# MLP matmuls in array tiles, and the ELU on two PSUM banks at once

## What is computed

```python
x = x + _L0_conv_ref(_gn(x), ...)   # 3x3 convolution, kernel mixed per sample from 3 experts
x = x + _L1_conv_ref(_gn(x), ...)   # abs, then a depthwise 3x3 convolution
x = x + _L2_conv_ref(_gn(x), 8)     # 17x17 box mean
x = x + _L3_conv_ref(_gn(x), ...)   # sum of 8 neighbours, then an MLP for each pixel
```

```python
nbr = _neighbor_sum(x_cat)
xn = jnp.repeat(nbr, 8, axis=1)
h = elu(w1 @ xn); h = elu(w2 @ h); h = elu(w3 @ h); h = elu(w4 @ h)
F_int = w5 @ h                      # then means over groups of 4, times 0.1
```

## Time and profile before

| | |
|---|---|
| median of three executions | 961.74 us |
| span of the profiled execution | 960.3 us |
| the profiled execution's own time | not listed apart from its span |
| PE busy | 827.8 us, 86% |
| DVE busy | 760.5 us, 79% |
| ACT busy | 628.2 us, 65% |
| POOL busy | 227.6 us, 24% |

### The profile page before, as it was taken

How to read it: one execution, slowest core, us unless ns; L and a number is a source line. 1 busy time by engine, 2 the same in 40 slices (tenths; PEclk the granted TensorE clock), 3 DMA queues, 4 the chain that set the end, 5 groups by cost and what they waited for, 6 DMA issues and landing times.

```text
span 960.3 us, 9306 instructions
## 1 busy us (share of the span) xinstructions
PE 827.8 (86%) x2391; PEld 397.9 (41%) x2391; DVE 760.5 (79%) x1267; ACT 628.2 (65%) x1105; POOL 227.6 (24%) x296
## 2 busy tenths in 40 slices
PE   2759786688999899998999899989998998979993
PEld 1423443353444345443445344444444452424330
DVE  2645674767989888988888898989897689878994
ACT  1020213476877768696878787787878687978883
POOL 2030143111512115122412151213312122221000
PEclk9979887988999999999999999999999899999997
DMA  5425423414020320214020402032112002001201
GB/s 97 77 43 93 86 37 71 88 23 74 8 61 16 59 38 17 60 24 72 16 60 16 67 13 62 15 58 38 34 44 47 17 17 61 16 16 41 54 16 44
DMA packets 68751, 43.18 MB, mean 45 GB/s; under 512 B 5602, under 2 KB 62306, under 8 KB 68722
## 3 DMA queue, kind: packets, MB, share of 16 engines
q1 hardware_dynamic: 66976, 42.57, 23.0%
q10 hardware_dynamic: 1746, 0.27, 0.2%
HBM read 9.67 MB, written 8.39 MB: 19 GB/s over the span
## 4 chain that ended last, share of the span: by engine, by line
PE 34%; DVE 28%; ACT 13%; DMA 10%; issue 6%; SPq 5%; POOL 2%; DVEq 0%; ACTq 0%; POOLq 0%
PE pz L700 17%; DVE g L908 8%; PE pc L644 6%; DMA xs<-in_x_dram 5%; ACT u L577 5%; ACT u L586 5%; DMA halo<-y 4%; DVE bn L828 4%; SPq L395 3%; DVE box_sum L961 3%; DVE u L903 3%; PE pc L659 3%; DVE box_sum L946 2%; ACT u L583 2%; PE pc L672 2%
## 5 line engine op out<-in xcount | busy, mean ns | idle before, releaser
L700 PE MATMUL pz<-g,wT 128*128 128x512 f32 x768 | 362.6, 611 | 11.7 <-DVE g L908 9.6
L577 ACT ACTIVATE u<-pz,s_row 128x512 f32<-128x512 f32 x354 | 241.6, 686 | 123.2 <-PE pz L700 121.9
L908 DVE SCALAR_TENSOR_TENSOR g<-pz,k_row,u 128x512 f32<-128x512 f32 x348 | 247.4, 744 | 57.2 <-ACT u L586 55.7
L586 ACT ACTIVATE u<-u 128x512 f32<-128x512 f32 x472 | 286.5, 635 | 1.3
L700 PEld LDWEIGHTS pz<-g,wT 128*128 128x128 f32 x768 | 144.9, 194 | 203.2 <-issue 113.2
L828 DVE BATCH_NORM_STATS2 bn<-xs 128x6 f32 (+1 forms) x128 | 87.1, 688 | 29.7 <-DMA xs<-in_x_dram 19.8
L696 PE MATMUL pz<-stack,w1T 128*128 128x512 f32 x256 | 83.8, 448 | 20.2 <-DMA stack<-near_rest 12.8
L659 PE MATMUL pc<-y,t 128*128 128x512 f32 x192 | 93.5, 625 | 5.2 <-DVE t L365 5.2
L669 PE MATMUL pc<-y,t 128*128 128x512 f32 x192 | 92.7, 620 | 2.4 <-ACT y L551 2.4
L577 ACT ACTIVATE u<-pz 128x512 f32<-128x512 f32 x118 | 68.2, 602 | 39.8 <-PE pz L696 39.8
L908 DVE SCALAR_TENSOR_TENSOR g<-pz,u 128x512 f32<-128x512 f32 x128 | 81.9, 683 | 11.3 <-ACT u L586 10.3
(11 more groups left out here) (118 smaller groups left out, 785.2 us busy)
## 6 DMA issues: line engine op xcount, KB each, us to landing
halo<-y SPq DMA_DIRECT2D x96, 120.0 KB, 3.3
xs<-in_x_dram SPq DMA_DIRECT2D x8, 1024.0 KB
stack<-near_rest SPq DMA_DIRECT2D x64, 128.0 KB, 2.3
out_dram<-xs SPq DMA_DIRECT2D x8, 1024.0 KB
stack<-stack SPq DMA_DIRECT2D x32, 128.0 KB, 2.2
halo<-y SPq DMA_DIRECT2D x48, 8.0 KB, 2.6
g<-in_con_late_dram SPq DMA_DIRECT2D x1, 712.5 KB, 9.6
con<-in_con_early_dram SPq DMA_DIRECT2D x1, 272.5 KB, 14.7
```

Source lines behind the costliest of these rows:

```text
L577: act.activation(u[:, m, :], pz[:, m, :], ACT.Relu, scale=-1.0, bias=s_row[:, l - 1:l] if l else 0.0).then_inc(relu_done, 1)
L586: act.activation(u[:, m, :], u[:, m, :], ACT.Exp, scale=-1.0).then_inc(exp_done, 1)
L700: pe.matmul(pz[:, m, :], wT[:, l - 1, :], g[:, m, :], start=True, stop=True).then_inc(z_mm, 1)
L908: dve.scalar_tensor_tensor(out=elus(j, q, l)[:, m, :], in0=pz[:, m, :], scalar=k_row[:, l - 1:l] if l else 1.0, in1=u[:, m, :], op0=ALU.ad ...
```

## The change

Layer 1 reads `near` itself: four float32 matmuls whose weights and data lie on 32 partitions each, one for each bank. The split on POOL, the three DMAs for each chunk, and the tiles `stack` and `near_rest` are gone. Layers 2 to 4 use the 64 by 64 weights without the zero blocks: for each pair of banks four matmuls, one in each quadrant of the array. Hidden vectors therefore change places between two banks in each layer. The output layer is four matmuls of 64 columns in two column groups, two of them adding to the other two.

The ELU works on a pair of banks (128 by 1024): relu, exp, relu, exp on ACT and two joins on DVE for each layer, with one semaphore step for each pair. `clips`, and the carrying of a join into the next chunk that went with it, are gone. The last layer's joins always write a tile of their own, `g_last`. The box and the neighbour sums share one pair of `band_part` tiles. DVE's `output` stands behind the joins of the next chunk's first layer everywhere.

```diff
-            def layer(j, q, l):
-                for m in range(M):
-                    if l == 0:
...
-                        if m == 0:
-                            pe.wait_ge(stack_in, STACK * (Q * j + q + 1))
-                        for n in range(2):
-                            last = pe.matmul(pz[:, m, :], w1T[n][:, m, :], stack[m // 2][:, :], start=n == 0, stop=n == 1)
-                        last.then_inc(z_mm, 1)
-                    else:
-                        pe.wait_ge(g_written, zn(j, q, l - 1, m))
-                        pe.matmul(pz[:, m, :], wT[:, l - 1, :], g[:, m, :],
-                                  start=True, stop=True).then_inc(z_mm, 1)
+            def first_layer(j, q):
+                if q > 0:
+                    pe.wait_ge(g_written, zn(j, q - 1, LAYERS - 1, 1))
+                elif not (isinstance(j, int) and j == 0):
+                    pe.wait_ge(g_written, zn(j - 1, Q - 1, LAYERS - 1, 1))
+                pe.wait_ge(conv_evac[3], Q * j + q + 1)
+                for m in range(M):
+                    rows = slice(32 * m, 32 * m + 32)
+                    last = pe.matmul(pz[:, m, :], wT[rows, 0, :], near[rows, q * CH:(q + 1) * CH], start=True, stop=True)
+                    if m % 2:
+                        last.then_inc(z_mm, 1)
+            def hidden_layer(j, q, l):
+                top, bottom = slice(0, HID), slice(HID, P)
+                for h in range(2):
+                    a, b = 2 * h, 2 * h + 1
+                    pe.wait_ge(g_written, zn(j, q, l - 1, h))
+                    pe.nop(nofuse=True)
+                    for rows, to in ((top, a), (bottom, b)):
+                        for half, of in ((top, a), (bottom, b)):
+                            last = pe.matmul(pz[half, to, :], wT[rows, l, rows], g[rows, of, :], start=True, stop=True)
+                    last.then_inc(z_mm, 1)
...
-                for m in range(M):
-                    last = pe.matmul(po[32 * m:32 * m + 32, :], w5T[:, :], elus(j, q, LAYERS - 1)[:, m, :],
-                                     start=True, stop=True)
+                for odd in range(2):
+                    for h in range(2):
+                        last = pe.matmul(po[HID * h:HID * h + HID, :], w5T[:, odd, :], g_last[:, 2 * h + odd, :],
+                                         start=odd == 0, stop=odd == 1)
```

```diff
             def elu(j, q, l):
...
-                    relu(0)
-                    for m in range(1, M):
-                        relu(m)
-                        exp(m - 1)
-                    exp(M - 1)
+                for h in range(2):
+                    pair = slice(2 * h, 2 * h + 2)
+                    act.wait_ge(z_mm, zn(j, q, l, h))
+                    act.activation(u[:, pair, :], pz[:, pair, :], ACT.Relu, scale=-1.0,
+                                   bias=s_row[:, l - 1:l] if l else 0.0).then_inc(relu_done, 1)
+                    act.wait_ge(relu_done, zn(j, q, l, h))
+                    act.activation(u[:, pair, :], u[:, pair, :], ACT.Exp, scale=-1.0).then_inc(exp_done, 1)
...
+            def joins(j, q, l):
+                for h in range(2):
+                    dve.wait_ge(exp_done, zn(j, q, l, h))
+                    pair = slice(2 * h, 2 * h + 2)
+                    dve.scalar_tensor_tensor(out=elus(l)[:, pair, :], in0=pz[:, pair, :], scalar=k_row[:, l - 1:l] if l else 1.0,
+                                             in1=u[:, pair, :], op0=ALU.add, op1=ALU.max).then_inc(g_written, 1)
```

```diff
             def round_box(i, c):
                 act.wait_ge(box_rows, Q * i + c + 1)
                 if c == 0 and not (isinstance(i, int) and i == 0):
-                    act.wait_ge(conv_mm[2], Q * i)
+                    act.wait_ge(conv_mm[3], Q * i)
             def round_near(i, c):
                 act.wait_ge(near_rows, Q * i + c + 1)
-                if c == 0 and not (isinstance(i, int) and i == 0):
-                    act.wait_ge(conv_mm[3], Q * i)
+                if c == 0:
+                    act.wait_ge(conv_mm[2], Q * i + Q)
```

More of the change, by code:

```diff
@@ L116, in build @@
         near = sb("near", [P, N])
-        near_rest = sb("near_rest", [P, CH], F32R)
-        stack = [sb(f"stack{n}", [P, CH], F32R) for n in range(2)]
         u = sb("u", [P, M, CH])
         g = sb("g", [P, M, CH])
+        g_last = sb("g_last", [P, M, CH])
         u_flat = u[:, :, :].rearrange("p m n -> p (m n)")
@@ L155, in build @@
         fcb = sb("fcb", [P, EXPERTS])
-        w1T = [sb(f"w1T{n}", [P, M, P], F32R) for n in range(2)]
-        wT = sb("wT", [P, 3, P])
-        w5T = sb("w5T", [P, 32])
+        wT = sb("wT", [P, 4, P])
+        w5T = sb("w5T", [P, 2, HID])
         s_row = sb("s_row", [P, 4])
@@ L258, in build, with zn, elus @@
         LOAD = 16
[L260 to L298, removed]
+        def zn(j, q, l, h):
+            return j * (Q * LAYERS * 2) + (q * LAYERS + l) * 2 + h + 1
+        def elus(l):
+            return g_last if l == LAYERS - 1 else g
         LAYER = (0, 2, 1, 3)
@@ L748, in _ @@
             pe.wait_ge(setup_dve, 2)
-            for n in range(M + 3):
+            for n in range(4):
                 last = pe.transpose(pz[:, :, :].rearrange("p a n -> p (a n)")[:, n * P:(n + 1) * P], wnat[:, n, :], const("ident"))
@@ L756, in _ @@
             for l in range(3):
-                pe.matmul(po[:, 64 + l:65 + l], wT[:, l, :], const("one"), start=True, stop=True)
-            for m in range(M):
-                last = pe.matmul(po[32 * m:32 * m + 32, 67:68], w5T[:, :], const("one"), start=True, stop=True)
+                pe.matmul(po[:, 64 + l:65 + l], wT[:, 1 + l, :], const("one"), start=True, stop=True)
+            for odd in range(2):
+                for h in range(2):
+                    last = pe.matmul(po[HID * h:HID * h + HID, 67:68], w5T[:, odd, :], const("one"), start=odd == 0, stop=odd == 1)
             last.then_inc(setup_pe, 1)
@@ L970, in one @@
                         if mlp:
-                            last = part_before(t, p) if l == 0 else None
-                            if last and not apart(*last):
-                                output(*last)
-                            elu(t - 1, p, l)
-                            if last and apart(*last):
-                                output(*last)
+                            joins(t - 1, p, l)
+                            if l == 0 and part_before(t, p):
+                                output(*part_before(t, p))
                         if l == norm_at(p, conv, mlp) and prev and prev[0] != 3:
```

146 lines of the change are left out of this document (32 added, 114 removed).

## The result

The changed kernel takes 979.03 us in the median of 4 runs (972.28 to 984.4), the kernel before 962.32 on the same chip: a ratio of 1.0187, with a 95% interval from 1.0118 to 1.0255. It is slower, clear of noise though by less than the 2% that the forecast called a change; the forecast was 957 and no change. One of the four executions of before took 1212.97 us and is not in the ratio. The profiled execution took 984.4 us, of which 982.6 are its span, 22.3 more than the span of before; its mean granted clock is 0.893 against 0.952.

What follows compares the result with a forecast made beforehand. PE was taken to set the pace. Rounds 1 to 6 (-33.7), start (-2.7), round 7 (+7.2), round 8 (+19.3) and clock (+5) gave -4.9: span 955.4, median 957 us; 8 in 10 range 905 to 1000.

Steps and rivals of the forecast that it cites:

- TensorE's clock: Rounds 7 and 8: PE works 9 of 22 us, idling nearly 4 at each chunk's end; 5 us added.
- Rival 2: Clock drops for good where PE is lightly loaded, in rounds 7, 8 and parts 1, 3: 994 us; chance 0.15.
- PE's groups: Layers 2 to 4: two groups of 1.1 us each, 1.35 to the relu; layer 1 takes 1.6 to its relu.
- ACT and DVE: Each layer's ELU on pairs: ACT 4.2 us, only 0.2 saved; DVE's joins 2.4 against 2.7.
- The ring: A pair's lap through ACT, DVE and PE: 4.9 us before the same pair's next relu.
- Chunk end and round 8: MLP alone: 7.2 us between relus over a chunk's end, 21.9 a chunk, 87.6 for round 8.
- The +19.3: Round 8: four chunks of 21.9 us make 87.6 against 68.3 now, so 19.3 us longer.
- Round 7: Its parts of 22.4, 23.0, 24.0 and 23.2 make 92.6 us against 85.4 now: +7.2.
- Part 0: In a clean round, 25.4 us against 28.1, with DVE's 24.0 us of work setting 6.0 a step: -2.7.
- costs nothing unless PE is the bound: Output layer: its second group adds 1.0 us on PE for each of 32 chunks, hidden behind layer 1.
- Parts 1, 2 and 3: In a clean round: 23.0 and 22.7 for parts 1 and 3, together +3.0; 29.2 for part 2, -2.2.
- The start: Before round 1, layer 1's wait of 2.7 us for its first stack goes: -2.7.

Runs made afterwards that it cites:

- experiment 13: Changed kernel with unread matmuls in PE's gaps of rounds 7 and 8 and ahead of layer 1 of every part 0: 961.68 us, 0.9996 of before.
- experiment 4: Changed kernel with unread matmuls on PE in round 8 only, behind each group and ahead of layer 1: 965.34 us, 1.0012 of before.
- experiment 8: Kernel before with only the stacking removed, layer 1 as four 32-row tiles each waiting for its own bank: 974.39 us, 1.0116 of before.
- experiment 3: Changed kernel with the ELU on single banks of 512 elements again, PE still working on pairs: 965.98 us, 1.003 of before.
- experiment 6: Changed kernel with the ELU on single banks and unread matmuls in PE's gaps of rounds 7 and 8: 954.49 us, 0.991 of before.
- experiment 11: Changed kernel with single-bank ELU, unread matmuls in rounds 7 and 8, and DVE doing each pair's second relu in round 8: 951.23 us, 0.9872 of before.
- experiments 14: Kernel of experiment 13 with half the output layer (the odd banks' share) left out: 973.82 us, 1.0121 of before.

## Why the prediction was wrong

The step that failed is the last of the sum, TensorE's clock: I added 5 us, for rounds 7 and 8 alone. Filling PE's pauses in the changed kernel was worth 17 us in the medians (979.03 to 961.68, experiment 13), and the clock was still not full then (0.953). With 17 in place of 5 the forecast of 957 becomes 969. The other 10 us up to 979 are terms of their own, below. Without its clock term the forecast is 952, against the 961.68 of experiment 13. In spans that is 950.4 against 959.1: the start 3.9 over the forecast, rounds 1 to 6 7.9 (six times 100.3 forecast) and round 7 1.1, less 4.2 for round 8 and what follows. That 979 still lies in the range of 905 to 1000 is owed to the range's width.

- *Where the clock falls.* The forecast named the light ends of parts 1 and 3 and the chunk ends of rounds 7 and 8. Parts 1 and 3 of round 3 kept 1.00; parts 0 of rounds 1 to 4 did not (0.89 to 0.90), and those of rounds 2 to 4 lost 3.3 us each. The clock is at half twice in each of these, and each time costs 1.7 us. The first is at the start: PE pauses 2.14 us ahead of layer 1 and then has only narrow work, and the output layer is caught. The second is at the end: PE pauses 1.30 us for the sums of the normalisation, has only tiny matmuls for them, and the last chunk of stage 0 is caught (4.52 us). In round 5 neither came (1.94 and 2.82):

```profile
363.78 1.14 PE L590 MATMUL pz<-near,wT 32*128 32x512 f32 x8 [2.14 <-DVE g_last L812]
364.85 3.41 PE L617 MATMUL po<-g_last,w5T 128*64 128x512 f32 x8
...
387.98 0.38 PE L526 MATMUL psm<-ms,con 128*128 128x2 f32 x2 [1.30 <-DVE ms L744]
...
388.67 4.52 PE L555 MATMUL pc<-y,t 128*128 128x512 f32 x6
...
575.59 1.94 PE L617 MATMUL po<-g_last,w5T 128*64 128x512 f32 x8
...
597.76 2.82 PE L555 MATMUL pc<-y,t 128*128 128x512 f32 x6
```

The same pause of 2.14 us in round 5 (574.51) brought no fall, nor did one of 2.15 in round 3 of experiment 4; what decides between the two was not found.

- *Rival 2* had the mechanism and the sign, and a size (37 us over the forecast) that was too large; I gave it 0.15 because round 8 of before ran at 1.00. That was the flaw: the clock of before was read with before's load on PE (62.76 of 70.9 us), and the change itself takes that load away. The Trainium skill, TensorE: Matmul & The Clock Gate, Why this matters for your kernels, asks that PE have no long idle gaps between bursts. Round 8 agrees (pauses of 3.63, clock 0.65, and 1.00 once they are filled); experiment 8 shows a fall with no idle time recorded ahead of it.
- *PE's groups.* A group is 1.09 us (1.1 forecast), from its start to the relu 1.15 (1.35), layer 1 to its relu 1.17 (1.6: 363.78 to 364.95 in round 3), the output layer 0.9 longer (1.0). The Trainium skill, TensorEngine Tiling (Array Packing), Key Properties, would have each change of tiling mode drain the engine; no price of that shows: in round 5 stage 0's first full-width matmul starts 1.86 us behind the start of the output layer's 1.94. The few tenths for each step that the prediction names beside this rule are shown by no run.
- *ACT and DVE.* Relu to exp 1.15 (1.14), exp to next relu 0.96 (0.95), join 1.28 (1.25), from its start to the next group 1.43 (1.30). The ring is 4.82 (4.9).
- *Chunk end and round 8.* At full clock a chunk is 21.1 us where 21.9 was forecast, and round 8 is 84.5 where it was 87.6; the shorter time from layer 1 to its relu, with the 1.15 of a group, is the difference. The +19.3 had a second error: the 68.3 it was taken from ends 2.6 us before round 8 does. Hand-offs cost 13.6. *Round 7*: 93.68 at 0.95, 92.6 forecast.
- *Part 0.* Forecast 25.4 in the mean of a clean round, measured 28.4 in the mean of six: 18 us in all. At full clock the six would be 25.35 (round 1 of experiment 13), four times 26.86, and 24.96 (round 6), which is 5.4 over the forecast; the other 12.7 are the clock. Of the 5.4, 4.3 are the output layer, five times 0.85, as no output layer stands ahead of the first part 0. That leaves 1 unexplained. That it "costs nothing unless PE is the bound" was right and wrongly applied: the sum had 5.8 us a step for PE without it, against 6.0 for DVE, and DVE turned out at 22.4 us of work and not 24.0.
- *Parts 1, 2 and 3.* 23.0 in the mean of six parts 1 (23.0 forecast), 22.6 in parts 3 (22.7), 29.8 in parts 2 (29.2).
- *The start.* The 2.7 us for the first stack did not come back: layer 1 starts at 154.91 (154.80 before). Something ahead of it ends as late; it varies from kernel to kernel with the same prologue (152.2 in experiment 3, 156.0 in 13), and what sets it was not followed.
- *Removing the stacking.* Taken out of the kernel before alone it gives +1.2% (experiment 8) and not the gain of 12.8 us that its waits suggested.

So the two ideas of the change pull apart. The 64x64 tiles are good for some 45 us under pairs. ELU on pairs costs 13 as measured (experiment 3), and 5 to 7 once both kernels have their clock held up. The idle PE that both leave costs some 17 until it is filled. Single banks and unread matmuls turn the change into a small gain (experiment 6), and with the clips it is 1.3% (experiment 11).

## What to carry to other kernels

Before an engine's work is cut, ask what clock the remaining work will be granted: cost the lightened stretches at both levels, full and half, and take neither from the profile of the busier kernel. Where one piece goes round three engines and nothing else fills them, as in round 8, the length of each instruction is on the path, and merging two small ones lengthens the lap though it lowers ACT's and DVE's busy shares; compare the laps (4.8 us for pairs, 4.5 for single banks), not the shares. In rounds 1 to 6, where other stages fill the engines, it made no difference that shows. An experiment that takes PE work away measures the clock too, and must hold it up to measure the work. And where the clock falls in one execution and not in the next, take the medians of several for the price, and a profile only for the place.

## What was not expected of the hardware

- Unread matmuls on an otherwise pausing PE made the whole kernel faster: round 8 went from 94.8 to 84.5 us, with the clock from 0.65 to 1.00, and the median from 979.0 to 965.3.
- Less work on PE made it slower: half the output layer less gave 973.8 us for 961.7 (experiments 14 and 13). In the changed kernel itself it gave 985.4 for 979.0, which is not clear of noise.
- The same code had its clock fall in one execution and not in another: rounds 1 to 6 took 622.9 and 612.8 us.
- Behind four 32-row tiles with waits between, the clock fell without any idle time of PE in the profile (3.08 us of tiles, then 3.89 for 2.84). The same tiles in one go take 1.14 us.
- A 64-column output in two accumulating groups takes 1.94 us, its first group alone 1.08 (eight and four records).
